# A four-block kernel on one core: the last 107 row transfers of the second expert layer, paced by a pause in place of a count of finished products

## The chip, the cores and the metric

One core of one Trainium2 chip, with its engines TensorE (PE, and PEld for weight loads), VectorE (DVE), ScalarE (ACT), GpSimd (POOL) and the queue engine SyncE (SP). The metric is the device time of one execution in microseconds. All arithmetic is in float32.

## The reference, cut to what matters

An activation x of 32 x 256 tokens with 128 features goes through four residual blocks, each behind a layer norm: a graph layer with gates, an expert layer with one expert of eight per token, a graph layer with two mixings and four small LSTMs of 1 to 4 steps, and an expert layer with two experts of eight per token. The change lies in the last one:

```
logits = flat @ router_w.T
probs = softmax(logits)
topk_probs, topk_idx = top_k(probs, 2)
topk_probs = topk_probs / (sum(topk_probs) + 1e-09)
h1 = einsum('nc,ehc->neh', flat, w1)
h3 = einsum('nc,ehc->neh', flat, w3)
h = silu(h1) * h3
y = einsum('neh,ech->nec', h, w2)
out = einsum('ne,nec->nc', gates, y)
x = x + out
```

Only the two chosen experts of a token are computed by the kernel.

## The kernel before, in words

The 8192 tokens are 64 tiles of 128 and stay in SBUF as `X`. In the second expert layer each token is written twice, once per chosen expert, into the DRAM table `expert_in`, sorted by expert. The table has 136 tiles of 128 rows (`NS` = 136), here called slots, in 17 groups of eight (`ND2` = 17).

The work on slot i:

- SP loads a group of eight slots (L537). TensorE transposes it in two halves (L1434), ACT copies the halves out (L964).
- TensorE makes six products, the two up projections in three parts each (L1444), and signals `d2_h`: one for each slot.
- ACT puts the SiLU on the first projection (L1034) behind a wait on `d2_h`, and copies the weights of a slot four further on (L957). The expert's number is read from a table (L951).
- DVE multiplies with the second projection (L2245) and signals `d2_m`; TensorE's up products of slot i + 2 wait for that (they use the same PSUM banks), and so do the down products of slot i (L1454).
- The result, scaled by the token's gate, is copied out of PSUM by ACT for the first 52 slots (L1000) and by DVE for the others (L2174). Either signals `d2_yo`. It stands in a ring of seven buffers `yd` of eight slots each.
- POOL sends the slot home: an indirect DMA (L712, `rows_home`) scatters its 128 rows of 512 bytes into the DRAM table `expert_out`, each to the place of its token.

At last SP reads that table back in ten blocks (L556), DVE adds the two rows of each token to `X` (L2202), and SP stores the result (L562). The first blocks are read when the groups that can hold their rows are home (`d3_ready`: 11, 13 and 17 groups).

POOL's instructions for this layer are in the order in which they are written. It sends rows 0 to 23 home, writes 32 x 2 half tiles of the second batches of tokens into `expert_in` around rows 24 to 28 (L731, `rows_in(1)` and `rows_in(2)`), and then sends rows 29 to 135 home: the 107 transfers of the change. Two kinds of gates set their times. Each has its own wait, for `d2_yo` to reach i + 1. Beside it the loop holds each one until the layer's progress `d2_h` has reached `min(68 + 5 * (i - 29) // 8, 136)`; 68 is `HOME_REST`. Other loops of indirect transfers have such counts too: L731 in this layer without anything else, the transfers of the first expert layer (L677, L706) and of the LSTM stretch (L687) with a `pause()` between the count and the transfer.

```
def pause():
    step(pool.memset(pause_p[:, :], 0.0))
```

`step` adds a signal to the instruction and lets POOL wait for it. The pause is a memset of one element in each partition (L659).

Of the kernel before, what the change touches and what calls it, by code (L numbers as in the profile page):

```python
# [55 lines left out]
def build(nc, x, adj_t, bias_io, gate_w, gate_b, w1, b1, wg, bg, wd, bd, g0_w, g0_b, g1_w, g1_b, wih_t, whh_t, bih, bhh,  # L56
# [30 lines left out]
    with ExitStack() as ctx:  # L87
# [3 lines left out]
        def sem(name):  # L91
            return ctx.enter_context(nc.semaphore(name))
# [200 lines left out]
        def flat(v):  # L293
# [50 lines left out]
        LG_AT = {i + 1: g for i, g in R_AT.items()}  # L344
        ROUTE_AT = {1: 16, 2: 32}
        RANK_STEP, RANK_COPY_STEP = 4, 5
        HOME_FIRST, LN_AT, IN_AT, HOME_MORE, HOME_REST = 24, (3, 7), (27, 48), 29, 68


        ND2 = NS // 8  # L350
# [4 lines left out]
        d2_tr, d2_xt, d2_h, d2_silu, d2_m, d2_y, d2_yo = (  # L355
            sem("d2_" + n) for n in "tr xt h silu m y yo".split())
# [225 lines left out]
        def _(pool):  # L582
            def step(ins):
                ins.then_inc(pool_step, 1)
                n_pool[0] += 1
                pool.wait_ge(pool_step, n_pool[0])
# [71 lines left out]
            def pause():  # L658
                step(pool.memset(pause_p[:, :], 0.0))  # L659
# [50 lines left out]
            def rows_home(i):  # L710
                pool.wait_ge(d2_yo, i + 1)
                pool.indirect_dma_start(  # L712
                    out=expert_out, out_offset=bass.IndirectOffsetOnAxis(ap=slot_row[:, i:i + 1], axis=0),
                    in_=yd[i // 8 % RING][:, i % 8, :], in_offset=None).then_inc(d2_out[i // 8 % RING], 16)
# [29 lines left out]
                rows_home(i)  # L744
            rows_in(2)
            for i in range(HOME_MORE, 8 * ND2):
                pool.wait_ge(d2_h, min(HOME_REST + 5 * (i - HOME_MORE) // 8, 8 * ND2))
                rows_home(i)


# [1 line left out]
        def _(act):  # L752
# [197 lines left out]
            def load_experts(first):  # L950
                _, r = nc.values_load_multi_w_load_instructions(  # L951
                    tile_e[0:1, bass.ds(first, 1)], engines=[ACT_ENGINE], min_val=0, max_val=E - 1,
                    skip_runtime_bounds_check_because="clamped to the last expert where it is computed")
                return r[0]
# [103 lines left out]
        def _(pe):  # L1058
            def load_experts(first, n):
                _, r = nc.values_load_multi_w_load_instructions(  # L1060
                    tile_e[0:1, bass.ds(first, n)], engines=[PE_ENGINE], min_val=0, max_val=E - 1,
                    skip_runtime_bounds_check_because="clamped to the last expert where it is computed")
                return r
# [447 lines left out]
        def _(dve):  # L1511
# [506 lines left out]
            def b2_dve(g, k, u, first, last):  # L2018
                if isinstance(g, int) and g == NB2 - 1:
                    g_norm(0, 0)  # L2020
                    g_norm(0, 1)
                _, er = nc.values_load_multi_w_load_instructions(
                    tile_e[0:1, bass.ds(4 * g, 4)], engines=[DVE_ENGINE], min_val=0, max_val=E - 1,
                    skip_runtime_bounds_check_because="clamped to the last expert where it is computed")
                dve.wait_ge(b2_y, g + 1)
                if not known_below(g, 2):
                    dve.wait_ge(b2_out[u], 16 * k)
                for j in range(4):
                    ins = dve.tensor_tensor(yb[u][:, j, :], bank[6 + u][:, j * P:(j + 1) * P],
                                            bd_sb[:, bass.ds(er[j] * D, D)], ALU.add)  # L2030
                ins.then_inc(b2_yo, 1)

                ahead_of_end = NB2 - g if isinstance(g, int) else NB2
                if 2 <= ahead_of_end <= 5:
                    for t in range((5 - ahead_of_end) * NH // 4, (6 - ahead_of_end) * NH // 4):
                        b3_tile(t)
                if ahead_of_end == 2:
                    b3_finish(0)
# [275 lines left out]
```

## Time and profile before

| what | us |
|---|---|
| median of three runs | 1142.44 |
| lowest, highest | 1140.64, 1149.63 |
| the profiled execution's own time | 1131.68 |
| its span | 1129.8 |
| TensorE busy in the span | 1019.6 |
| POOL busy in the span | 500.0 |

The profile is of one execution and its times are microseconds from the start of the span. A row of the timeline names start, duration, engine, line of the kernel, operation, what is written and read, the count of merged instructions, and in brackets the idle time of the engine before it with what ended it. "issue" there is time in which the engine waited for nothing that the profile shows, "remote" a releaser that the profile could not name. The ends of matmuls are modelled. A row of the windows names a stretch, its length, the busy time of each engine asked for with the count of its instructions, then TensorE's granted clock as a share of full speed, the share of the DMA engines, and GB/s.

### The profile page before, as it was taken

Reading aid. Unit: us, or ns where it says so; the run is one execution under the profiler, and the core shown is the slowest. Engines: PE = TensorE matmul, PEld = TensorE weight load, DVE = VectorE, ACT = ScalarE, POOL = GpSimd, SP = SyncE. Lnnn points to the kernel's source line nnn. Section 1 sums busy time; section 2 is a strip of 40 time slices with the busy share of each in tenths; the row PEclk is TensorE's granted clock in tenths of the full one; section 3 lists DMA queues with packets and bytes.
Section 4 is the critical chain, followed back from the end, with each engine's and each line's share of the span. In section 5 each row is a group of like instructions: output and inputs, shape, how many; then the busy total and the mean of one; then the engine's idle time right before and its main releaser. Section 6 shows DMA issues by size and latency. Waiting matters only on the chain.

```text
span 1129.8 us, 17682 instructions
## 1 busy us (share of the span) xinstructions
PE 1019.6 (90%) x5432; PEld 714.9 (63%) x5433; DVE 600.5 (53%) x1829; ACT 617.1 (55%) x1158; POOL 500.0 (44%) x831
## 2 busy tenths in 40 slices
PE   5799985999898899999999999999997899989893
PEld 2344432677667544654685456448997798889892
DVE  7977894411165265654765774436474533333365
ACT  4677852544332485664336766656766555454550
POOL 5852275731734420000120058745346666666652
PEclk9899987999998999999999999999998899999997
DMA  9850012332323130000000001131112222222447
GB/s 276 350 221 1 0 45 64 96 105 70 104 68 84 32 119 0 1 1 0 1 1 1 1 31 46 49 86 37 44 46 64 65 83 66 81 63 84 186 159 223
DMA packets 79876, 86.29 MB, mean 76 GB/s; under 512 B 10114, under 2 KB 65970, under 8 KB 79026
## 3 DMA queue, kind: packets, MB, share of 16 engines
q1 hardware_dynamic: 67250, 59.28, 16.6%
q0 software_dynamic: 12544, 25.98, 7.0%
q8 instruction: 44, 0.72, 0.3%
q14 instruction: 38, 0.31, 0.1%
HBM read 40.64 MB, written 44.58 MB: 75 GB/s over the span
## 4 chain that ended last, share of the span: by engine, by line
PE 65%; DVE 13%; ACT 7%; another core or an unknown queue 6%; issue 5%; DMA 2%; POOL 1%; ACTq 1%; DVEq 0%; POOLq 0%; SPq 0%
PE bank L1417 16%; PE bank L1444 14%; PE bank L1424 8%; PE bank L1454 4%; PE bank L1293 3%; PE bank L1181 3%; PE bank L1152 2%; PE bank L1333 2%; PE bank L1361 2%; ACT sb_whh_sb L957 2%; PE bank L1118 1%; PE bank L1322 1%; PE bank L1350 1%; ACTq L951 1%
## 5 line engine op out<-in xcount | busy, mean ns | idle before, releaser
L1417 PE MATMUL bank<-sb_R,sb_wih_sb 128*128 128x512 f32 (+2 forms) x504 | 197.8, 543 | 1.2 <-issue 1.2
L977 ACT ACTIVATE sb_R<-bank,sb_lb_sb 128x512 f32<-128x512 f32 (+2 forms) x252 | 153.4, 634 | 73.7 <-PE bank L1424 61.3
L712 POOL DMA_INDIRECT expert_out<-sb_R,sb_slot_row x136 | 132.5, 974 | 114.6 <-ACT sb_R L1000 45.9
L2245 DVE TENSOR_TENSOR sb_R<-sb_R,bank 114x384 f32<-114x384 f32 x136 | 75.3, 554 | 183.4 <-ACT sb_R L1034 113.0
L1417 PEld LDWEIGHTS bank<-sb_R,sb_wih_sb 128*128 128x128 f32 x504 | 95.3, 190 | 96.4 <-issue 75.7
L1034 ACT ACTIVATE sb_R<-bank 114x384 f32<-114x384 f32 x136 | 66.4, 488 | 148.1 <-PE bank L1444 109.3
L1444 PE MATMUL bank<-sb_xt,sb_wih_sb 128*114 128x128 f32 x792 | 103.4, 282 | 22.4 <-DVE sb_R L2245 9.4
L1454 PE MATMUL bank<-sb_BIG,sb_R 114*128 x816 | 115.5, 278 | 1.3 <-issue 0.8
L1444 PEld LDWEIGHTS bank<-sb_xt,sb_wih_sb 128*114 128x114 f32 x792 | 94.3, 184 | 27.5 <-issue 25.1
L1424 PE MATMUL bank<-sb_R,sb_whh_sb 128*128 128x512 f32 (+2 forms) x288 | 111.1, 529 | 0.0
L1444 PE MATMUL bank<-sb_xt,sb_whh_sb 128*114 128x128 f32 x792 | 99.3, 275 | 5.7 <-ACT sb_wih_sb L957 5.7
L1454 PEld LDWEIGHTS bank<-sb_BIG,sb_R 114*128 114x128 f32 x816 | 103.2, 194 | 1.8 <-issue 1.6
L614 POOL TENSOR_TENSOR sb_ln_p<-sb_ST 128x8 f32<-128x8 f32 (+2 forms) x15 | 3.3, 221 | 221.6 <-DVE sb_ST L1659 162.3
L1444 PEld LDWEIGHTS bank<-sb_xt,sb_whh_sb 128*114 128x114 f32 x792 | 91.8, 179 | 7.9 <-issue 6.9
L659 POOL MEMSET sb_pause_p<- 128x1 f32 x192 | 21.6, 112 | 168.9 <-DVE sb_dest_i L1769 66.4
L901 ACT ACTIVATE sb_R<-bank,sb_b_sb 128x512 f32<-128x512 f32 x72 | 46.3, 688 | 83.3 <-PE bank L1152 75.0
L1424 PEld LDWEIGHTS bank<-sb_R,sb_whh_sb 128*128 128x128 f32 x288 | 54.7, 190 | 50.5 <-issue 35.6
L731 POOL DMA_INDIRECT expert_in<-sb_R,sb_dest_i x64 | 62.1, 970 | 40.4 <-PE bank L1444 17.3
L687 POOL DMA_INDIRECT expert_in<-sb_R,sb_dest_i x64 | 66.5, 1039 | 19.4 <-POOL sb_pause_p L659 11.8
L1293 PE MATMUL bank<-sb_BIG,sb_R 128*128 x576 | 67.8, 276 | 6.4 <-ACT sb_R L901 4.0
L1293 PEld LDWEIGHTS bank<-sb_BIG,sb_R 128*128 128x128 f32 x576 | 65.8, 192 | 8.0 <-issue 7.8
L677 POOL DMA_INDIRECT sorted_in<-sb_R,sb_dest_i x64 | 62.6, 978 | 17.8 <-issue 11.1
(308 smaller groups left out, 1757.6 us busy)
## 6 DMA issues: line engine op xcount, KB each, us to landing
sb_XS<-expert_in SPq DMA_DIRECT2D x17, 528.0 KB
expert_in<-sb_R SPq DMA_DIRECT2D x17, 512.0 KB, 6.3
sb_R<-expert_out SPq DMA_DIRECT2D x6, 1024.0 KB, 6.6
sorted_in<-sb_R SPq DMA_DIRECT2D x9, 512.0 KB, 5.3
sb_XS<-sorted_in SPq DMA_DIRECT2D x18, 256.0 KB
sorted_out<-sb_R SPq DMA_DIRECT2D x18, 256.0 KB
sb_X<-x SPq DMA_DIRECT2D x8, 512.0 KB, 7.5
out<-sb_X SPq DMA_DIRECT2D x6, 512.0 KB
```

Source lines behind the costliest of these rows:

```text
L677: pool.indirect_dma_start(out=sorted_in, out_offset=bass.IndirectOffsetOnAxis(ap=dest_i[:, 0, t:t + 1], axis=0), in_=XN[:, t, :], in_offse ...
L687: pool.indirect_dma_start(out=expert_in, out_offset=bass.IndirectOffsetOnAxis(ap=dest_i[:, k, t:t + 1], axis=0), in_=XR[:, t, :], in_offse ...
L712: pool.indirect_dma_start(out=expert_out, out_offset=bass.IndirectOffsetOnAxis(ap=slot_row[:, i:i + 1], axis=0), in_=yd[i // 8 % RING][:, ...
L731: pool.indirect_dma_start(out=expert_in, out_offset=bass.IndirectOffsetOnAxis(ap=dest_i[:, k, t:t + 1], axis=0), in_=XR[:, t - NH, :], in_ ...
L977: act.activation(gb[s][k][:, 0:c], bank[4 * s + k][:, 0:c], funcs[k], bias=lb_sb[:, (p - 1) * GATES + k:(p - 1) * GATES + k + 1]).then_inc ...
L1034: act.activation(sl[j % 2][0:HC, :], bank[2 + 2 * (j % 2)][0:HC, 0:KU * P], ACT.Silu).then_inc(d2_silu, 1)
L1293: mm = pe.matmul(bank[6 + u][:, j * P:(j + 1) * P], Ht[u][:, c, j * P:(j + 1) * P], wd_sb[:, c, bass.ds(er[j] * D, D)], start=(c == 0 and ...
L1417: mm = pe.matmul(bank[4 * s + k][:, 0:c].rearrange("p (w b) -> p w b", b=GH), wih_sb[:, p - 1, k * P:(k + 1) * P], xin, start=True, stop=( ...
L1424: pe.matmul(bank[4 * s + k][:, 0:c], whh_sb[:, p - 1, k * P:(k + 1) * P], hst[s][:, 0:c], start=False, stop=True).then_inc(l_g, 1)
L1444: mm = pe.matmul(bank[2 + 2 * (j % 2) + part][0:HC, c * P:(c + 1) * P], weights_of(i)[:, part * UP + c * HC:part * UP + (c + 1) * HC], xt[ ...
L1454: mm = pe.matmul(bank[6 + j % 2][:, 0:D], hm[j % 2][0:HC, c * P:(c + 1) * P], down_sb[0:HC, bass.ds(expert * (KU * D) + c * D, D)], start= ...
L2245: dve.tensor_tensor(hm[j % 2][0:HC, :], sl[j % 2][0:HC, :], bank[3 + 2 * (j % 2)][0:HC, 0:KU * P], ALU.mult).then_inc(d2_m, 1)
```

## The change

The wait of each of the last 107 transfers for `d2_h` is taken away, with its constant. In its place stands a `pause()` ahead of the transfers 29 to 119; the last sixteen, 120 to 135 (`8 * (ND2 - 2)` is 120), have none. The wait for the own row, inside `rows_home`, stays.

```diff
--- before.py
+++ after.py
@@ -344,7 +344,7 @@
         LG_AT = {i + 1: g for i, g in R_AT.items()}
         ROUTE_AT = {1: 16, 2: 32}
         RANK_STEP, RANK_COPY_STEP = 4, 5
-        HOME_FIRST, LN_AT, IN_AT, HOME_MORE, HOME_REST = 24, (3, 7), (27, 48), 29, 68
+        HOME_FIRST, LN_AT, IN_AT, HOME_MORE = 24, (3, 7), (27, 48), 29
 
 
         ND2 = NS // 8
@@ -744,7 +744,8 @@
                 rows_home(i)
             rows_in(2)
             for i in range(HOME_MORE, 8 * ND2):
-                pool.wait_ge(d2_h, min(HOME_REST + 5 * (i - HOME_MORE) // 8, 8 * ND2))
+                if i < 8 * (ND2 - 2):
+                    pause()
                 rows_home(i)
```

On POOL's queue the place behind the last of the transfers into `expert_in` (L731) reads as follows. `expert_out` is the table of results, `sb_R` the ring of rows, and the names in brackets are the semaphores waited for; the lines with a minus are the kernel before.

```order
 L731 DMA expert_in<-sb_R,sb_dest_i 17408x132 [waits d2_h,d1_places]
 L731 DMA expert_in<-sb_R,sb_dest_i 17408x132 [waits d2_h] x31
-L712 DMA expert_out<-sb_R,sb_slot_row 33792x128 [waits d2_yo,d2_h] x107
+L659 MEMSET sb_pause_p 128x1
+L712 DMA expert_out<-sb_R,sb_slot_row 33792x128 [waits d2_yo,pool_step]
+L659 MEMSET sb_pause_p 128x1
+L712 DMA expert_out<-sb_R,sb_slot_row 33792x128 [waits d2_yo,pool_step]
```

The 107 transfers that stood as one row with a wait for `d2_h` are now pairs of a memset, which waits for nothing, and a transfer, which waits for the memset and for its own row.

At the end of POOL's queue, the last rows before its final branch are:

```order
+L659 MEMSET sb_pause_p 128x1
+L712 DMA expert_out<-sb_R,sb_slot_row 33792x128 [waits d2_yo,pool_step]
+L659 MEMSET sb_pause_p 128x1
+L712 DMA expert_out<-sb_R,sb_slot_row 33792x128 [waits d2_yo,pool_step]
+L712 DMA expert_out<-sb_R,sb_slot_row 33792x128 [waits d2_yo] x16
 L87 UNCONDITIONAL_BRANCH
```

The sixteen last transfers keep only the wait for their own row. The order of the instructions on the other four engines is as before.

## Rows read from the trace of the kernel before

**Rows 1.** The page: span, busy time by engine, the chain by line

```profile
span 1129.8 us, 17682 instructions
PE 1019.6 (90%) x5432; PEld 714.9 (63%) x5433; DVE 600.5 (53%) x1829; ACT 617.1 (55%) x1158; POOL 500.0 (44%) x831
PE bank L1417 16%; PE bank L1444 14%; PE bank L1424 8%; PE bank L1454 4%; PE bank L1293 3%; PE bank L1181 3%; PE bank L1152 2%; PE bank L1333 2%; PE bank L1361 2%; ACT sb_whh_sb L957 2%; PE bank L1118 1%; PE bank L1322 1%; PE bank L1350 1%;
```

**Rows 2.** Windows, SiLUs of the layer (L1034): us, ACT busy (count), clock, DMA

```profile
946.80:1090.00 143.20, 28.73 (x59) 1.00 0.30 100
```

**Rows 3.** Timeline: first transfer concerned, and SiLUs 67, 126 and 135

```profile
946.80 0.96 POOL L712 DMA_INDIRECT expert_out<-sb_R,sb_slot_row  x1 [1.10 <-PE bank L1444]
946.87 0.49 ACT L1034 ACTIVATE sb_R<-bank 114x384 f32<-114x384 f32 x1 [1.90 <-PE bank L1444]
...
1090.05 0.47 ACT L1034 ACTIVATE sb_R<-bank 114x384 f32<-114x384 f32 x1
...
1108.09 0.49 ACT L1034 ACTIVATE sb_R<-bank 114x384 f32<-114x384 f32 x1 [1.49 <-PE bank L1444]
```

**Rows 4.** Timeline of one burst, 1027 to 1032 us

```profile
1027.83 1.54 PE L1444 MATMUL bank<-sb_xt,sb_wih_sb 128*114 128x128 f32 x12 [1.47 <-ACT sb_whh_sb L957]
1029.04 0.96 POOL L712 DMA_INDIRECT expert_out<-sb_R,sb_slot_row  x1 [0.30 <-issue]
...
1031.10 0.96 POOL L712 DMA_INDIRECT expert_out<-sb_R,sb_slot_row  x1 [1.11 <-PE bank L1444]
1031.18 0.49 ACT L1034 ACTIVATE sb_R<-bank 114x384 f32<-114x384 f32 x1 [2.39 <-PE bank L1444]
```

**Rows 5.** Timeline without bursts, 1092 to 1094 us

```profile
1092.24 1.50 PE L1444 MATMUL bank<-sb_xt,sb_wih_sb 128*114 128x128 f32 x12
...
1094.11 0.49 ACT L1034 ACTIVATE sb_R<-bank 114x384 f32<-114x384 f32 x1 [0.86 <-PE bank L1444]
```

**Rows 6.** 841 to 851 us: windows of transfers (L731), of SiLUs (L1034); timeline

```profile
841.50:851.00 9.50, 7.31 (x8) 0.96 0.15 50
841.50:851.00 9.50, 0.98 (x2) 0.96 0.15 50
...
849.98 0.49 ACT L1034 ACTIVATE sb_R<-bank 114x384 f32<-114x384 f32 x1 [5.61 <-remote]
```

**Rows 7.** Windows to 946.8 us: rows out by ACT (L1000), by DVE (L2174)

```profile
755.00:946.80 191.80, 18.97 (x52) 0.95 0.20 60
755.00:946.80 191.80, 4.47 (x13) 0.95 0.20 60
```

**Rows 8.** Timeline with paused transfers, first expert layer, 172 to 176 us

```profile
172.32 0.11 POOL L659 MEMSET sb_pause_p<- 128x1 f32 x1
172.71 0.96 POOL L677 DMA_INDIRECT sorted_in<-sb_R,sb_dest_i  x1 [0.28 <-issue]
...
174.93 0.60 ACT L836 ACTIVATE sb_R<-bank 128x512 f32<-128x512 f32 x1 [6.45 <-remote]
175.58 0.69 PE L1209 MATMUL bank<-sb_ident,sb_R 128*128 128x128 f32 x2 [6.43 <-issue]
```

**Rows 9.** Timeline of the last transfer, and the chain behind it

```profile
1113.49 0.96 POOL L712 DMA_INDIRECT expert_out<-sb_R,sb_slot_row  x1 [0.30 <-issue]
1113.49 3.65 DMA expert_out<-sb_R,sb_slot_row
...
1117.39 4.25 DMA sb_R<-expert_out
```

**Rows 10.** Windows, a product of the first expert layer (L1181): PE, PEld, clock, DMA

```profile
111.70:152.30 40.60, 23.61 (x48) 7.57 (x46) 1.00 0.04 13
154.20:183.00 28.80, 11.60 (x20) 3.93 (x18) 0.70 0.20 66
```

**Rows 11.** LSTM stretch: windows (PE, PEld, DVE, ACT, POOL); POOL's transfers in lines

```profile
671.00:729.00 58.00, 58.00 (x179) 33.62 (x178) 26.47 (x48) 35.99 (x66) 45.79 (x80) 1.00 0.14 47
L687 POOL DMA_INDIRECT expert_in<-sb_R,sb_dest_i x40 | 41.3, 1032 | 12.0 <-POOL sb_pause_p L659 7.6 <-issue 4.4
```

## The prediction

> **What bounds the kernel now.** Read first the header of the page and the busy time of the last layer's stretches. TensorE is busy 1019.6 of 1129.8 us [rows 1]. The change touches only POOL's last 107 transfers, which run from 946.8 us on, so the question is what sets the pace of the second expert layer from there to the end. The chain of waits over the span puts 14% on L1444, the up product of this layer [rows 1]: TensorE's chain through the slots is what ends last, not POOL.
>
> Then count slots. One slot of 128 rows is one SiLU on ACT at L1034. Between 946.8 and 1090.0 us there are 59 of them [rows 2], and the last ten of the 136 come after. By the starts of slots 67, 126 and 135 (946.87, 1090.05 and 1108.09 us, [rows 3]) 59 steps take 143.2 us, 2.43 us each, and the last nine 18.0 us, 2.00 us each. TensorE's clock is granted in full meanwhile (1.00, its 2.4 GHz level, [rows 2]), so the 0.43 us per slot are waiting: 59 x 0.43 = 25 us.
>
> Where do they go? The timeline of a burst shows it [rows 4]. POOL issues three transfers 1.26 us apart (0.96 for one and 0.30 between), the third at 1029.04. The up product that starts at 1027.83 is over by about 1029.3, yet ACT, idle, starts its SiLU only at 1031.18, after 2.39 us of idleness. POOL, which waits for the same count of finished up products, is let go at 1031.10. So the signal of that product came at about 1031, some 1.7 us late and about 1 us after POOL's third transfer was done (1029.04 + 0.96 = 1030.00). This comes again in each burst. Where POOL sends one or two transfers and then rests, the product at 1092.24 (1.50 us) is answered at 1094.11, 0.4 us after its end [rows 5]. I call it a hold: during transfers in a row TensorE's signals reach nobody, and TensorE, which may be two slots ahead, then stands too. What bounds this stretch is TensorE's chain, and POOL's bursts stretch it. The price of a long burst without pauses is at 841 us: eight transfers in 10 us, beside them two SiLUs, and ACT idle for 5.61 us until 849.98 [rows 6].
>
> **The change, step by step.** *Removed:* POOL's wait for finished up products. At transfer 29 it asks for 68, the next ones for five more in every eight transfers, so bursts of three or four per two slots. At about transfer 125 the rule asks less than the row's own readiness does, and the wait is empty; that is the stretch after 1090. *Kept:* each transfer waits for its own row. Before 946.8 ACT and DVE have put out 52 + 13 = 65 rows [rows 7] and POOL has sent 29 home, so 36 rows are ready: for 36 transfers and more nothing at all stops POOL now.
>
> *Added:* 91 pauses (transfers 29 to 119), a memset of 0.11 us and its own signal. In the paused transfers of the first expert layer the spacing is 1.35 us (0.96 + 0.11 + 0.28, [rows 8]) against 1.26 us without. On POOL that is 91 x 0.09 = 8 us of issue, beside the layer's work as long as POOL is not last. 91 x 1.35 + 16 x 1.26 = 143 us is the least POOL needs; it now takes from 946.80 to 1113.49 + 0.96 = 1114.45, 167.7 us [rows 3, 9].
>
> *Moved:* every one of the transfers 30 to about 124 goes earlier. No other instruction moves on POOL, SP, PE, ACT or DVE. SP's first reads of the rows home wait until transfer 87 has landed, which would be some 946.8 + 59 x 1.35 + 3.65 = 1030 us; they write a region that nobody uses by then, and DVE adds what they bring at fixed slots (the first with 17 slots to go), so I cost their being earlier at nothing. The ring of seven row buffers gets emptier; at a lead of 36 of its 56 rows it was not full before either.
>
> Now the sum. The layer goes through two phases. In phase A POOL runs without stop at 1/1.35 = 0.741 transfers per us and eats its lead of 36 while slots take s us: A = 36 / (0.741 - 1/s). Then it sends one transfer per slot, as after 1090, and slots take 2.00 us. With 68 slots left, the stretch takes T = A + 2.00 x (68 - A/s). Now it takes 143.2 + 18.0 = 161.2 us. So all hangs on s, the slot under transfers with pauses and no stop, which no row shows in this layer. Bounds:
> - s = 2.00, a pause ends every hold: the layer takes 136 us, POOL with 143 us is last, and the end comes 167.7 - 143 = 25 us earlier.
> - s without end, nothing passes before POOL stands: T = 48.6 + 136 = 184.6, 23 us later.
> - s = 2.70 gives 161.2 back: no change.
> Nearest rows. (a) First expert layer, paused transfers in a row from 141 us on: the first product L1181 comes 48 times in 40.6 us before 152.3 us and 20 times in 28.8 us after 154.2 us [rows 10], 0.85 against 1.44 us, a factor 1.7; part of it is a clock of 0.70, itself from TensorE's idling. In it TensorE stands 6.43 us at 175.58 and ACT 6.45 us at 174.93, while POOL's paused transfers run on [rows 8]. 1.7 x 2.00 gives s = 3.4 and T = 169.1. (b) The burst of eight without pauses in this layer gives two SiLUs in 10 us [rows 6], s = 5, T = 175.9. (c) The 40 paused transfers of the LSTM stretch, 671 to 729 us, during which TensorE is busy 58.00 of 58.00 us [rows 11]: no hold at all, s = 2.00. Its products are long and two signals per slot do not hang on each other so tightly.
> I take s = 4, between (a) and (b): pauses were there in (a) and did not help, and this layer's chain leaves TensorE only two slots ahead, so it is nearer to (b) than an estimate by (a) says. A = 36 / 0.491 = 73.3 us, 18.3 slots, T = 73.3 + 99.4 = 172.7, which is 11.5 us more than 161.2. The tail from the last row home (3.65 us to land, 4.25 us to read, adds and stores, [rows 9]) stays. The span goes from 1129.8 to 1141.3 and the profiled execution from 1131.7 to 1143.2 us. That execution lies 10.8 us under the median of the runs, 1142.4; I add the same 11.5 us to the median: 1153.9, put as 1154.
>
> *A rule weighed.* The row shows ACT and TensorE idle beside POOL's transfers and let go when they stop [rows 4]. The Trainium skill, page "SBUF — State Buffer", section "Who interferes with whom", says that DMA never contends with a compute engine and that PE and ACT never wait on anyone. By that rule there is no hold, and the change could only take a wait off POOL, the first rival below. This case's trace disagrees as far as signals go, with 2.39 us of idleness in one burst; it doesn't say that SBUF ports are the cause.
>
> **Rivals.**
> 1. *The pause works* (faster). A memset and a wait on its own signal between two transfers leaves the signals a door, and the hold never forms, as in the LSTM stretch [rows 11]. Against it stand (a) and the 6.4 us [rows 8]. Then s = 2.0 to 2.4: T = 143 to 155, 6 to 25 us less; I price it at 18 less, 1124.
> 2. *Even trade* (no change). Holds form but open by themselves every three or four transfers, s = 2.4 to 2.9: T from 155 to 165, and the 0.43 us saved in phase B pay for phase A. 1142, give or take 6. For it: two slots per burst now already give 2.43.
> 3. *Whole hold* (slower, more). No signal passes until POOL has used up its 36 rows: 48.6 us of standstill at 947 us, then 136 us: 1142 + 23 = 1165. For it: the bursts so far ended only when POOL stopped [rows 4]. Against it: at 849.98 and 174.93 the answer came while transfers ran [rows 6, 8].
> The side changes at s = 2.70.
> 4. That the change does nothing, the own row's wait taking the old wait's place at once, is excluded by the lead of 36 rows [rows 7].
>
> **Chances.** Forecast (s = 3 to 5, 5 to 15 us more): 0.45. Rival 1: 0.27. Rival 2: 0.18. Rival 3: 0.10. One per cent, 11.4 us, is about what a measurement of this kernel can tell from no change. Faster by over 1%: the larger part of rival 1, 0.23. Slower by over 1%: half and more of the forecast and all of rival 3, 0.44. Same: 0.33. The range reaches to 1120 (rival 1 nearly whole) and 1167 (rival 3 with a little over it); the forecast's own is 1147 to 1158.
>
> **What would show it.** Right: SiLUs from 947 us on in pairs with gaps of 5 us and more for some 70 us, some 18 slots in it; POOL's transfers 1.35 us apart with only 0.28 us idle; then slots of 2.00 us with one transfer each; the last SiLU near 1119 us. TensorE's idle time would sit in the first phase, and perhaps its clock falls to the lower level there, which the sum leaves out. Wrong, if slots are at 2.0 to 2.4 us right after 947 us (the pause works), if POOL waits for rows before 1000 us, or if the last transfer is late by itself, with the layer over by 1083 us and POOL still issuing.

## The result, and the profile after

| | kernel before | changed kernel |
|---|---|---|
| median | 1141.54 us | 1168.84 us |
| lowest to highest | 1137.81 to 1149.63 | 1162.08 to 1172.53 |
| ratio, 95% interval | | 1.024 [1.020, 1.028] |
| profiled execution's own time, span | 1131.68, 1129.8 | 1170.66, 1168.4 |

The changed kernel is slower by 2.4%, 27 us. The forecast was 1154, and its range ended at 1167. In the changed kernel the lines of the code stand one higher: L1034 is now L1035, L1444 is L1445, L2245 is L2246. POOL's lines keep their numbers.

The page of the changed kernel, against [rows 1]: span, busy time, the chain by engine, and the SiLUs' group.

```profile
span 1168.4 us, 17757 instructions
PE 1022.7 (88%) x5432; PEld 719.7 (62%) x5433; DVE 601.2 (51%) x1829; ACT 620.8 (53%) x1158; POOL 514.2 (44%) x922
...
PE 58%; DVE 12%; another core or an unknown queue 10%; POOL 7%; issue 6%; ACT 5%; DMA 2%; ACTq 0%; DVEq 0%; SPq 0%; POOLq 0%
...
L1035 ACT ACTIVATE sb_R<-bank 114x384 f32<-114x384 f32 x136 | 66.7, 490 | 174.5 <-PE bank L1445 98.8
```

TensorE does the same work, 1022.7 us against 1019.6, in a span that is 38.6 us longer: the time is waiting. A tenth of the chain (6% before) has no releaser that the profile can name; since the kernel has one core, that is a signal recorded long after the instruction that sent it.

Where it sits, by windows of 20 us of the changed kernel (busy time and count of PE, PEld, DVE, ACT, POOL, then clock, DMA share, GB/s):

```profile
940.00:960.00 20.00, 15.21 (x133) 14.54 (x131) 5.21 (x16) 8.70 (x16) 13.44 (x19) 1.00 0.26 75
960.00:980.00 20.00, 4.34 (x19) 4.11 (x20) 1.70 (x5) 1.16 (x2) 15.83 (x31) 0.59 0.14 47
980.00:1000.00 20.00, 6.00 (x22) 4.70 (x22) 0.01 (x1) 0.00 (x0) 15.45 (x29) 0.59 0.14 49
1000.00:1020.00 20.00, 10.60 (x74) 10.63 (x75) 4.32 (x14) 6.49 (x12) 9.10 (x19) 0.64 0.09 30
1020.00:1040.00 20.00, 20.00 (x184) 20.00 (x183) 8.32 (x25) 12.68 (x23) 10.56 (x20) 1.00 0.30 81
```

From 960 to 1000 us POOL alone works steadily. TensorE is busy 4 and 6 us of 20, and its granted clock is at the lower of its two levels for most of that time (0.59 on average); from 1020 us on it is busy all the time at full clock. The ACT timeline of the same stretch, against [rows 3]:

```profile
957.91 0.49 ACT L1035 ACTIVATE sb_R<-bank 114x384 f32<-114x384 f32 x1 [4.84 <-remote]
...
970.82 0.49 ACT L1035 ACTIVATE sb_R<-bank 114x384 f32<-114x384 f32 x1 [11.77 <-remote]
...
1001.84 0.49 ACT L1035 ACTIVATE sb_R<-bank 114x384 f32<-114x384 f32 x1 [29.86 <-issue]
...
1009.08 0.49 ACT L1035 ACTIVATE sb_R<-bank 114x384 f32<-114x384 f32 x1 [6.09 <-remote]
```

ACT stands idle 4.84, 11.77 and 29.86 us ahead of three SiLUs. Not all of an idle time is a late signal: the up product behind the SiLU at 1001.84 was over only at 982.69, so the SiLU came 19.1 us after it. VectorE waits too. The SiLU at 970.82 is over at 971.31, and its product comes 7.8 us later:

```profile
979.12 0.55 DVE L2246 TENSOR_TENSOR sb_R<-sb_R,bank 114x384 f32<-114x384 f32 x1 [16.36 <-remote]
```

VectorE needs two signals there, ACT's and TensorE's `d2_y` of an earlier down product, and the trace's own record of signals tells them apart. That `d2_y` is recorded at 979.02, 12.2 us after the end of its down product (966.81) and 0.1 us ahead of VectorE's row. Between 940 and 1010 us the trace has 12 signals of ACT and 8 of VectorE (it misses some), and each is recorded 0.01 us after the end of its instruction. Of TensorE's 17, 15 are recorded over 0.5 us late. So it is TensorE's signals that come late, to ACT, to VectorE and, in [rows 4], to POOL.

Nor is it signals alone. The six parts of the down product that comes last before the SiLU at 1001.84 wait for nothing that the profile shows, and yet come one at a time, the starts mostly 0.7, 1.4 or 2.1 us apart. The whole takes 8.1 us, where the six before it, also at the lower clock, took 1.49 us:

```profile
965.32 1.49 PE L1455 MATMUL bank<-sb_BIG,sb_R 114*128 x6
...
987.44 0.37 PE L1455 MATMUL bank<-sb_BIG,sb_R 114*128 x1 [1.84 <-issue]
988.17 0.37 PE L1455 MATMUL bank<-sb_BIG,sb_R 114*128 x1 [0.35 <-issue]
...
990.28 0.37 PE L1455 MATMUL bank<-sb_BIG,sb_R 114*128 x1 [1.74 <-issue]
...
995.20 0.37 PE L1455 MATMUL bank<-sb_BIG,sb_R 114*128 x1 [1.05 <-issue]
```

Meanwhile POOL, in the groups by line between 954 and 1006 us, waits for nothing but its own pauses (count | busy, mean ns | idle before):

```profile
L712 POOL DMA_INDIRECT expert_out<-sb_R,sb_slot_row x38 | 36.4, 957 | 11.5 <-issue 8.7 <-POOL sb_pause_p L659 2.8
L659 POOL MEMSET sb_pause_p<- 128x1 f32 x37 | 4.2, 113 | 0.0
```

At last the SiLUs alone, in the hold and in full flow:

```profile
954.19:1007.20 53.01, 1.47 (x3) 0.62 0.19 59
1017.70:1099.50 81.80, 19.19 (x40) 1.00 0.23 65
```

The sum of the stretch: the first of the 107 transfers goes at 954.19 (before: 946.80, so this execution was 7.4 us later ahead of the change's place), three slots pass until 1007, the fourth SiLU is at 1009.08, and the last one at 1146.86. That is 54.9 + 137.8 = 192.7 us, against 161.3 before: 31.4 us more. The tail behind the last SiLU is 21.5 us against 21.7. So 7.4 + 31.4 - 0.2 = 38.6 us, the difference of the two spans; the medians lie 27.3 us apart.

### The profile page after: what moved, and what is told of

The parts are those of the page before. It is cut to its first block, busy times and chain, and to the rows that moved or that the text cites. A ratio compares the mean times of both kernels' runs of the same rounds, so it can differ in the third digit from the quotient of the medians.

```text
span 1168.4 us, 17757 instructions
## 1 busy us (share of the span) xinstructions
PE 1022.7 (88%) x5432; PEld 719.7 (62%) x5433; DVE 601.2 (51%) x1829; ACT 620.8 (53%) x1158; POOL 514.2 (44%) x922
## 4 chain that ended last, share of the span: by engine, by line
PE 58%; DVE 12%; another core or an unknown queue 10%; POOL 7%; issue 6%; ACT 5%; DMA 2%; ACTq 0%; DVEq 0%; SPq 0%; POOLq 0%
PE bank L1445 14%; PE bank L1418 10%; PE bank L1455 7%; POOL expert_in L687 6%; PE bank L1425 4%; PE bank L1153 4%; PE bank L1294 3%; PE bank L1182 3%; PE bank L1334 2%; PE bank L1362 2%; PE bank L1119 1%; PE bank L1323 1%; PE bank L1351 1%; PE bank L1343 1%
## 5 line engine op out<-in xcount | busy, mean ns | idle before, releaser
L712 POOL DMA_INDIRECT expert_out<-sb_R,sb_slot_row x136 | 136.6, 1004 | 131.5 <-DVE sb_R L2175 56.1
L2246 DVE TENSOR_TENSOR sb_R<-sb_R,bank 114x384 f32<-114x384 f32 x136 | 75.3, 554 | 217.6 <-remote 69.9
L1035 ACT ACTIVATE sb_R<-bank 114x384 f32<-114x384 f32 x136 | 66.7, 490 | 174.5 <-PE bank L1445 98.8
L1455 PE MATMUL bank<-sb_BIG,sb_R 114*128 x816 | 118.7, 281 | 9.2 <-issue 8.7
L1445 PE MATMUL bank<-sb_xt,sb_wih_sb 128*114 128x128 f32 x792 | 105.2, 286 | 23.5 <-DVE sb_R L2246 18.9
L1445 PE MATMUL bank<-sb_xt,sb_whh_sb 128*114 128x128 f32 x792 | 100.4, 277 | 27.4 <-DVE sb_R L2246 13.8
L1445 PEld LDWEIGHTS bank<-sb_xt,sb_wih_sb 128*114 128x114 f32 x792 | 97.9, 189 | 25.3 <-issue 23.3
L1455 PEld LDWEIGHTS bank<-sb_BIG,sb_R 114*128 114x128 f32 x816 | 105.9, 197 | 10.2 <-issue 10.1
L1445 PEld LDWEIGHTS bank<-sb_xt,sb_whh_sb 128*114 128x114 f32 x792 | 93.6, 182 | 29.1 <-issue 29.1
L659 POOL MEMSET sb_pause_p<- 128x1 f32 x283 | 31.8, 112 | 172.7 <-DVE sb_dest_i L1770 72.6
L902 ACT ACTIVATE sb_R<-bank,sb_b_sb 128x512 f32<-128x512 f32 x72 | 46.7, 687 | 82.7 <-PE bank L1153 70.7
L1425 PEld LDWEIGHTS bank<-sb_R,sb_whh_sb 128*128 128x128 f32 x288 | 54.7, 190 | 50.5 <-issue 36.4
L731 POOL DMA_INDIRECT expert_in<-sb_R,sb_dest_i x64 | 62.0, 969 | 43.8 <-PE bank L1445 18.3
L1182 PE MATMUL bank<-sb_xt,sb_w_sb 128*128 128x512 f32 x128 | 69.0, 636 | 4.7 <-ACT sb_R L831 4.4
```

The costliest lines, as they stand in the source:

```text
L712: pool.indirect_dma_start(out=expert_out, out_offset=bass.IndirectOffsetOnAxis(ap=slot_row[:, i:i + 1], axis=0), in_=yd[i // 8 % RING][:, ...
L731: pool.indirect_dma_start(out=expert_in, out_offset=bass.IndirectOffsetOnAxis(ap=dest_i[:, k, t:t + 1], axis=0), in_=XR[:, t - NH, :], in_ ...
L1035: act.activation(sl[j % 2][0:HC, :], bank[2 + 2 * (j % 2)][0:HC, 0:KU * P], ACT.Silu).then_inc(d2_silu, 1)
L1182: pe.matmul(bank[2 + c % 2][:, :], w1_sb[:, c * P:(c + 1) * P], xt[b // 2 % 2][:, b % 2 * BANK:(b % 2 + 1) * BANK], start=True, stop=True) ...
L1425: pe.matmul(bank[4 * s + k][:, 0:c], whh_sb[:, p - 1, k * P:(k + 1) * P], hst[s][:, 0:c], start=False, stop=True).then_inc(l_g, 1)
L1445: mm = pe.matmul(bank[2 + 2 * (j % 2) + part][0:HC, c * P:(c + 1) * P], weights_of(i)[:, part * UP + c * HC:part * UP + (c + 1) * HC], xt[ ...
```

## Experiments

### Two conditions

One fact came with the first comparison and is needed for all that follows. The kernel before takes two times that lie 61 to 77 us apart. Within a comparison it keeps to one of them, with a spread of 2 to 14 us:

| comparison | chip | kernel before, us | kernels |
|---|---|---|---|
| first, with the result | | 1141.54 | changed |
| A | 5 | 1068.29 | bare, both, gap128, two |
| B | 5 | 1068.20 | before_again, after_again |
| C | 5 | 1144.92 | nopause |
| D | 6 | 1129.08 | bare2, gap128b |
| E | 8 | 1138.68 | two2, both2, mem36, dir36 |
| F | 9 | 1139.39 | gap256, sort2, gath2 |
| G | 7 | 1067.83 | sort2b, combo |

I call them the free condition (A, B, G) and the held one. Chip 5 showed both. Every ratio below is to the kernel before in the same comparison.

### Both kernels again

No edit: each kernel as it stood.

> The kernel before, unchanged, for a trace of it where its time is what the last four runs were compared with (1068.3 us, not 1141.5). Theory C (the holding back of signals while GpSimd issues transfers 1.26 to 1.35 us apart belongs to the chip or the session, not to the kernel): no hold in any row of transfers, every slot of the second expert layer 1.98 us with one of 2.42 in four, mean 2.09, and 1068 us. Theory K (it comes and goes from one execution to the next): holds here too, and times that differ by tens of us between runs.

> The changed kernel, unchanged, compared again. Theory C: no hold here, so nothing is lost: GpSimd needs 91 x 1.35 + 16 x 1.26 = 143 us, about what the layer needs (131 us) plus the tail, and the ratio is that of the version with wait and pause, 1.000 to 1.006. Theory K: a hold of some 50 us at the first 36 transfers and a ratio near 1.02 as first measured.

Measured: 1068.19 us, and 1071.17, a ratio of 1.0031 [1.0021, 1.0041]. That is theory C and not K, and by comparison C, on the same chip, it is not the chip. The kernel before, in the free condition: all engines from the first transfer to the last SiLU, then the SiLUs alone, against [rows 2].

```profile
906.70:1044.50 137.80, 137.80 (x1255) 137.80 (x1254) 65.86 (x179) 81.99 (x146) 100.73 (x103) 1.00 0.41 136
```

```profile
906.73:1044.50 137.77, 32.61 (x67) 1.00 0.41 136
```

Rows of POOL and ACT from its timeline:

```profile
930.73 0.96 POOL L712 DMA_INDIRECT expert_out<-sb_R,sb_slot_row  x1 [0.30 <-issue]
...
931.94 0.49 ACT L1034 ACTIVATE sb_R<-bank 114x384 f32<-114x384 f32 x1 [0.80 <-PE bank L1444]
931.99 0.96 POOL L712 DMA_INDIRECT expert_out<-sb_R,sb_slot_row  x1 [0.30 <-issue]
...
933.25 0.96 POOL L712 DMA_INDIRECT expert_out<-sb_R,sb_slot_row  x1 [0.30 <-issue]
...
933.92 0.49 ACT L1034 ACTIVATE sb_R<-bank 114x384 f32<-114x384 f32 x1 [0.83 <-PE bank L1444]
```

Transfers stand 1.26 to 1.29 us apart, 92 in a row, and nothing is held: 67 slots, 2.08 us from one SiLU to the next, with TensorE busy all the time. Between the first transfer and the last SiLU the trace has 148 signals of TensorE, and each is recorded within 0.01 us of its instruction's end; in the held execution, from 946.8 to 1090 us, 76 of 115 are over 0.5 us late. The removed wait stopped none of these 92 transfers; it can have stopped only some of the last fifteen, which go at the pace of the slots. Both executions of the kernel before reach their 166th us within 0.3 us of each other; by the starts of ACT's instructions, each beside its like, the held one falls behind wherever indirect transfers come in rows (the first goes at 142 us): 17.5 us by 380 us, 0.9 us in the LSTM stretch, and the rest in the second expert layer: 63.7 us between the spans of 1129.8 and 1066.1.

In the free condition the change costs what POOL's pauses cost. Its last transfer is at 1055.16 against 1049.87, 5.3 us later, the wait behind it is 1.8 us shorter, and the span 3.5 us longer.

### Without wait and without pause

```diff
-                if i < 8 * (ND2 - 2):
-                    pause()
```

> The changed kernel without its 91 pauses: the last 107 transfers of rows home in the second expert layer have neither the wait nor a pause ahead of them, so GpSimd issues them 1.26 us apart, not 1.35. Theory H (a row of such transfers holds back the signals of the other engines as long as it lasts, pause or no pause): the hold lasts from transfer 29 to about 65, 36 x 1.26 = 45 us instead of the 49 to 52 us of the changed kernel, and the time is 0 to 6 us below the changed kernel's, 1162 to 1169 us. Theory P (the pause instruction itself, a write to SBUF, is what holds): the hold is gone and the time is within 5 us of the kernel before, 1137 to 1147 us.

> The version without wait and without pause again, since the kernel before has shown both of its times (1068 and 1145 us) in comparisons an hour apart. Where before takes about 1068 us again: the same as before, as the first time. Where it takes about 1141 to 1145 us: Theory H (the whole lead of 36 transfers holds the signals, pause or none, and only the end of the row lets them go) gives a hold of 36 x 1.26 = 45 us, a first-transfer-to-last-SiLU stretch of about 45 + 8 (what was in flight) + 65 x 2.12 = 185 us and 1160 to 1170 us, ratio 1.015 to 1.025. Theory P (the pauses made it worse): ratio 1.00 to 1.01.

Measured: free 0.9997 [0.9982, 1.0012]; held 1.0247 [1.0205, 1.0288]. In the held one, SiLUs in the lead (windows) and the one that ends the hold (timeline):

```profile
942.30:989.00 46.70, 0.98 (x2) 0.61 0.20 64
```

```profile
994.38 0.49 ACT L1033 ACTIVATE sb_R<-bank 114x384 f32<-114x384 f32 x1 [37.35 <-remote]
```

Two slots in 46.7 us: as in the changed kernel, over 37 transfers 1.26 us apart. Here too TensorE's signals alone are recorded late (12 of 14 between 935 and 1000 us, none of ACT's 13 or VectorE's 7): the product behind the SiLU at 994.38 ended at 969.00, and its signal is recorded 25.0 us later. The changed kernel's loss is that of the wait removed; the pause of one element neither makes the hold nor breaks it. Theory P falls.

### Wait and pause together

```diff
                 pool.wait_ge(d2_h, min(HOME_REST + 5 * (i - HOME_MORE) // 8, 8 * ND2))
+                if i < 8 * (ND2 - 2):
+                    pause()
                 rows_home(i)
```

> The wait of the kernel before and the pause of the changed one together, ahead of the same transfers. Theory H: with the wait the transfers come in twos and singly, such short rows hold nothing, and a pause inside them adds nothing: within 3 us of the kernel before. Theory P (the pause itself is harmful): 91 pauses in the stretch cost at least 0.1 us each, slower by 9 us or more. If, a third way, the pause does some good once rows are short, the 2.4 us slots of the kernel before shrink towards 2.1 us and it is faster by up to 59 x 0.3 = 18 us.

> The wait of the kernel before and the pause together, again. Where before takes about 1068 us: 1.003 again. Where it takes 1129 to 1145 us: if what holds is the third and fourth transfer of a row, and at 1.35 us a row holds as at 1.26 us, slots stay at 2.43 us and the ratio is 0.998 to 1.004; if 0.09 us more between transfers already eases the hold in short rows, up to 59 slots x 0.3 us less, ratio down to 0.985.

Measured: free 1.0032 [1.0019, 1.0044], held 1.0038 [1.0014, 1.0062]. In the held one 68 slots take 169.7 us against 69 in 161.3 before. With short rows the pause brings nothing and costs 4 to 5 us.

### How far apart

The pause is written over more elements (128 or 256 of each partition), or made twice:

```diff
-                    pause()
+                    long_pause()     # pool.memset(pause_p[:, :], 0.0), pause_p of 128 or of 256 columns
```

> The changed kernel with each of the 91 pauses written over 128 elements of each partition instead of one, so that the transfers should be about 1.45 us apart instead of 1.35. Theory T (there is a spacing from which a row of transfers no longer holds the signals; in the LSTM stretch rows 1.40 to 1.49 us apart held nothing): the hold is gone, the stretch from the first of the transfers to the last SiLU is set by the layer or by GpSimd, 68 x 2.1 = 143 us against 91 x 1.45 + 16 x 1.26 = 152 us, so about 10 us faster than the kernel before. Theory H (any row held close together holds, whatever the small gap): the lead of 36 transfers lasts 36 x 1.45 = 52 us plus what the layer gets done, and the time is that of the changed kernel plus 3 to 6 us.

> The version with transfers 1.46 us apart again. Where before takes about 1068 us: 1.012 again. Where it takes about 1141 to 1145 us: Theory T (from some spacing on a row holds nothing; rows 1.35 to 1.49 us apart held nothing in the LSTM stretch, rows 1.26 us apart did) gives slots of 2.12 us from the first transfer on, GpSimd last at 91 x 1.46 + 16 x 1.26 = 153 us, and 8 to 10 us less than before, ratio 0.99. Theory H: a hold of 36 x 1.46 = 53 us, 1168 to 1176 us, ratio 1.02 to 1.03. In between (s slots per us of hold as I had chosen it for the prediction, s = 4) the ratio is 1.01.

> The changed kernel with a wider pause, two of the short ones in a row ahead of each of the 91 transfers: spacing between 1.45 and 1.75 us. Theory T: no hold; the slots are 2.1 us from the start, the layer ends about 143 us after the first transfer, and GpSimd ends last if the spacing is 1.74 us (91 x 1.74 + 16 x 1.26 = 178 us, 17 us slower than before) or with the layer if it is 1.45 us. Theory H: the hold lasts 36 transfers, 52 to 63 us, and the time is at least that of the changed kernel.

> Transfers 1.84 us apart, again. Where the kernel before takes about 1068 us: ratio 1.045 again. Where it takes 1129 to 1145 us: if the hold gets less with the spacing (1.26 and 1.35 us: no slot gets through; 1.46 us: one in 3.8 us), slots here take 2.1 to 2.4 us from the first transfer on, GpSimd ends last, 192 us from first to last transfer against 167 us before, ratio about 1.02. If spacing does not matter beyond 1.46 us: slots of 3.8 us in the lead, and 1.03 or more.

> The changed kernel with each of the 91 pauses written over 256 elements of each partition: about 1.60 us between transfers. Where the kernel before takes 1129 to 1145 us: if the hold ends below 1.60 us, slots of 2.12 us from the first transfer on, GpSimd last after 91 x 1.60 + 16 x 1.26 + some 4 us for the columns' steps = 170 us against 166.7 us before, ratio 1.000 to 1.003. If it ends between 1.60 and 1.84 us: slots of 2.5 to 3.8 us in the lead, 1.003 to 1.015. Where it takes about 1068 us: GpSimd last, 170 against 143 us, ratio 1.025.

The SiLUs of the layer, windows in the lead, of the versions with 128 columns, with 256, and with two pauses, all held:

```profile
940.30:1024.00 83.70, 10.76 (x22) 0.86 0.21 65
```

```profile
948.29:980.00 31.71, 5.91 (x12) 0.95 0.27 78
948.29:1103.50 155.21, 33.51 (x69) 0.99 0.37 121
```

```profile
950.17:1060.00 109.83, 25.58 (x53) 1.00 0.24 71
```

| spacing, us | kernel | slot in the lead, held | ratio, held | ratio, free |
|---|---|---|---|---|
| 1.26 | bare | 2 in 46.7 us | 1.0247 [1.0205, 1.0288] | 0.9997 [0.9982, 1.0012] |
| 1.35 | changed | 3 in 53.0 us | 1.024 [1.020, 1.028] | 1.0031 [1.0021, 1.0041] |
| 1.46 | gap128 | 3.80 us | 1.0149 [1.0112, 1.0185] | 1.0125 [1.0098, 1.0151] |
| 1.57 | gap256 | 2.64 us | 0.9994 [0.9966, 1.0022] | not tried |
| 1.84 | two | 2.07 us | 1.0180 [1.0132, 1.0227] | 1.0447 [1.0419, 1.0474] |

The hold is a matter of spacing. Below 1.4 us two or three slots get through in some 50 us, at 1.46 a slot takes nearly twice its time, at 1.84 it takes what it takes in the free condition. The other side of it is POOL: at 1.84 us it ends last, at 1144.49 in the held run, 45 us behind the last SiLU, and so at every spacing from 1.35 on in the free condition, where the end comes 14.4 to 14.7 us behind the last transfer. (In both versions with two pauses one slot waits 8 to 14 us: DVE's addition L2204, ahead of the slot's product in its order, waits for rows that POOL sends so late.) Theory H, any close row holds alike, falls. Theory T was right in kind, but not at 1.46, where I had put the end of the hold from the LSTM stretch.

### What in the row holds

The changed kernel with transfers 29 to 64, the lead, replaced. Both leave those rows of the result out; two copies in the LSTM stretch fill them.

```diff
+                if HOME_MORE <= i < HOME_MORE + 36:      # mem36
+                    for k in range(4):
+                        step(pool.memset(pause_p[:, :], 0.0))    # 256 columns
...
+                if HOME_MORE <= i < HOME_MORE + 36:      # dir36
+                    pool.dma_start(out=dump[(i - HOME_MORE) * P:(i - HOME_MORE + 1) * P, :],
+                                   in_=yd[i // 8 % RING][:, i % 8, :]).then_inc(d2_out[i // 8 % RING], 16)
```

> The changed kernel, in which transfers 29 to 64 of the rows home (the 36 of the lead) are left out and four writes of 256 elements of GpSimd's own, each waited for, stand in their place, so that GpSimd stays about as busy but moves nothing; two copies in the LSTM stretch fill the rows that are then not written. Theory D (the transfers hold the signals): no hold in the lead, slots of 2.0 to 2.1 us from the first on also where the kernel before takes 1129 to 1145 us, and 12 to 50 us less than the changed kernel there, ratio to before 0.97 to 0.99. Theory B (GpSimd busy without a stop holds them, whatever it does): the hold of 45 to 52 us remains, ratio about 1.02.

> The changed kernel, in which the same 36 transfers go with the same bytes from the same buffers, on GpSimd's queue, but to rows in order of a buffer of their own instead of the rows that an index names; the same two copies fill the rows not written. If scattering by index is what holds: no hold in the lead, ratio to before 0.97 to 0.99 where before takes 1129 to 1145 us. If any transfer that GpSimd issues holds: as the changed kernel, ratio about 1.02. Where before takes about 1068 us all of this shows nothing and the ratio is 1.00 to 1.01.

Measured, both held: 1.0236 [1.0196, 1.0276] and 1.0063 [1.0025, 1.0100]. By the ratio alone mem36 would be theory B; the windows say otherwise. SiLUs of mem36 beside the memsets and from the first indirect transfer on, then one of its ACT rows there:

```profile
965.00:1023.50 58.50, 13.71 (x28) 1.00 0.16 40
1023.50:1070.00 46.50, 2.45 (x5) 0.65 0.18 58
```

```profile
1061.13 0.49 ACT L1049 ACTIVATE sb_R<-bank 114x384 f32<-114x384 f32 x1 [18.95 <-remote]
```

SiLUs of dir36 beside the direct transfers and after them, and POOL's group of direct transfers:

```profile
964.70:999.60 34.90, 8.33 (x17) 1.00 0.38 117
999.60:1036.00 36.40, 3.43 (x7) 0.72 0.14 45
```

```profile
L715 POOL DMA_DIRECT2D dump<-sb_R x36 | 19.5, 541 | 11.2 <-POOL sb_pause_p L661 11.2
```

Beside POOL's own writes (1.35 us busy of each 1.63) slots take 2.09 us, and beside direct transfers, 36 in 34.9 us with a DMA share of 0.38, 2.05 us. (Windows of this length miss part of a slot; from SiLU to SiLU both are 2.1 us.) As soon as the indirect ones begin, 1.35 us apart, the signals are held: five slots in 46.5 us, seven in 36.4. The hold had only moved: behind the replaced part 34 indirect transfers went without a stop in mem36 and 21 in dir36, against 38 in the changed kernel. That fits the ratios. So what holds, in the held condition, is the row of indirect transfers, not POOL being busy and not DMA traffic. The direct transfers differ from the indirect ones in more than one thing (0.54 us of POOL against 0.96, targets in order), and I did not part these.

### The pauses already there, and rows of the sort

nopause takes the pauses of the kernel before out; sort2 doubles them ahead of the rows that the sort scatters and gathers, gath2 of the gathered ones alone; combo is sort2 and gap256 together.

```diff
             def pause():
-                step(pool.memset(pause_p[:, :], 0.0))
+                pass                                 # nopause
...
                     pause()
+                    pause()                          # sort2: in scatter_b and gather; gath2: in gather
```

> The kernel before without any of its 192 pauses (ahead of the rows scattered in the sort, the rows gathered and the rows scattered in the LSTM stretch); everything else, the wait for the layer's progress too, as before. Theory C (transfers in a row hold nothing where the kernel before takes 1068 us, and something where it takes 1141 us): where before takes 1068 us, the pauses buy nothing, GpSimd is not last in those stages, and the time is within 3 us of before. Where before takes 1141 us, the rows of 1.26 us hold at least as much as those of 1.35 us did (17.4 us lost by the sort's stage), so the same or slower. Theory Q (the pauses already in the kernel are what keeps the signals going where it takes 1068 us): slower than before by 10 us or more, also there.

> The kernel before with two pauses instead of one ahead of each of the 64 rows that the sort scatters and the 64 that it gathers, 1.84 us apart instead of 1.35; the second expert layer as before. Where before takes 1129 to 1145 us: the holds between 150 and 350 us, which cost 17 us, go; against it stands GpSimd's own time, 64 x 0.49 = 31 us more in a stage of 105 us, if the layer has to wait for its rows. Between 17 us less and 14 us more; I take 5 us less, ratio 0.995. Where before takes about 1068 us: 0 to 14 us more.

> The same for the gathered rows alone (64 of them, the first 32 in a row). Where before takes 1129 to 1145 us: the 8 us of hold between 277 and 325 us go and nothing waits for the gathered rows soon after, ratio 0.993; if the gathers are not what held there, 1.000. Where before takes about 1068 us: 1.000.

> The kernel before with two pauses ahead of each scattered and gathered row of the sort, again. Where before takes 1129 to 1145 us: ratio 0.993 as the first time (0.990 to 0.997). Where it takes about 1068 us, where no row holds anything: the rows come 0.16 us later each, 64 x 0.16 = 10 us in a stage that has room for it or not, ratio 1.000 to 1.009.

> Both: two pauses in the sort, and in the second expert layer no wait but a pause of 256 elements (transfers 1.57 us apart). Where before takes 1129 to 1145 us: the sort's gain alone, since GpSimd ends last in the second layer whatever the layer does, 0.9934 x 0.9994 = 0.993; if the two add more than that, because the layer and GpSimd now end close together, 0.985. Where it takes about 1068 us: GpSimd last, 1.025.

nopause, held: 1.0155 [1.0085, 1.0225]. Rows 1.26 us apart now hold in the LSTM stretch too, where rows from 1.35 us on had held nothing [rows 11]: windows of all engines, TensorE 51.78 of 60 us.

```profile
660.00:720.00 60.00, 51.78 (x162) 31.75 (x161) 25.72 (x55) 28.16 (x56) 38.74 (x39) 0.91 0.13 43
```

By the starts of ACT's instructions, each beside the same one of the free execution, this version loses 17.3 us in that stretch and the kernel before 0.9. There 0.09 us of pause are worth some 16 us, while the same pause in the second expert layer is worth nothing. nopause was not tried in the free condition, so theory Q stays untested. sort2 (1.51 us apart): held 0.9934 [0.9897, 0.9971], free 1.0111 [1.0095, 1.0126]. gath2, held: 0.9984 [0.9964, 1.0003], no difference. In the profiled execution of sort2 I don't find the gain at its place, TensorE being busy 200.6 us of 145 to 370 us against 199.6 before, so where its 7 us come from stays open. combo, free: 1.0341 [1.0327, 1.0355]; its layer runs at 2.08 us per slot and POOL ends last at 1088.19, 31.6 us behind the last SiLU. I could not try it held. So one version beats both kernels, by 0.7%, in the held condition alone, and it loses 1.1% in the free one.

## Why the prediction was wrong

*What bounds the kernel: right.* TensorE's chain of slots bounds the stretch, held up by its own signals while POOL's rows go out. The free condition shows the size of it: 2.08 us from SiLU to SiLU, against 2.37 in the held one (68 steps in 161.2 us). The prediction put the waiting at 0.43 us per slot over 59 slots, 25 us; measured against 2.09, the step without holds, it is 0.34 us and 20 us.

*The lead of 36: right.* POOL sent 38 transfers 1.35 us apart without waiting, to 1006 us, and then about one for each slot.

*The moved reads, the tail: right.* They cost nothing, 21.5 against 21.7 us.

*The failed step: "I take s = 4, between (a) and (b)".* It measured 3 slots in 53 us, so s was over 17 and the hold as good as whole. That was rival 3, which had a chance of 0.10. The reasoning failed in two places. (b), two SiLUs beside eight transfers [rows 6], was read as a rate. In bare2 and the changed kernel it is a start: two SiLUs come in the first 14 and 17 us of the row and then none for 38 and 31 us, so dividing a short burst by its slots gives a rate that a long row does not have. And (a), the first expert layer, mixes spacings: [rows 10] covers transfers of which some are 1.5 to 1.9 us apart, and the series above shows that this tenth of a microsecond decides. s = 3.8 is what the layer shows at 1.46 us. I had asked whether the pause opens the door, and not how wide the gap must be. The prediction also took a hold to be late signals alone; the traces show TensorE's own instructions slowed as well, 8.1 us for a down product.

*A mis-sized term: "slots take 2.00 us" in phase B.* Nine slots at the layer's end gave it, [rows 3]. They hold one group of transposes, where full flow has one in each four slots. In full flow of the changed kernel 40 steps from SiLU to SiLU, from 1017.77 to 1101.40 us, take 83.6 us, 2.09 each (the window above, which ends ahead of the last of them, makes it look like 2.05); with the slots right behind the hold 65 took 137.8 us, 2.12 each. Against 2.00 that is 8 us. Rival 3 with it is 184.6 + 8 = 192.6 us, and 192.7 was measured; that it fits so closely is luck, since the hold lasted 54.9 us and not 48.6, and three slots got through in it. Rival 3 had been priced at 1165 us, inside the range; the measured median lies 2 us above the range, less than these 8 us.

*Rival 1, the pause works:* not at 1.35 us. Two pauses in a row do it (2.07 us per slot), and then POOL is last: the 143 us that I had as POOL's least belong to a spacing of 1.35, and at 1.84 it needs 194.

*Rival 2, even trade:* not at 1.35 us either. A trade that comes out even is gap256, 1.57 us apart, 0.9994.

*The rule weighed.* Read as the prediction read it, that nothing is held, the rule doesn't fit the held condition: a SiLU came 19.1 us after its product. The Trainium skill, "SBUF — State Buffer", "Who interferes with whom", speaks of SBUF ports; by that rule POOL's own writes would not disturb TensorE or ACT, and neither would direct DMA, and mem36 and dir36 agree with both (2.1 us per slot). The free condition agrees with it altogether. Had I trusted it, I would have said faster, and in neither condition was the changed kernel faster.

*What stays open.* Why an execution is held or free. The kernel, its work to the 166th us and the number and bytes of its DMA packets are the same, and chip 5 showed both. What the chip's other cores did meanwhile is not on record, and no run here tells whether that, or the recording of the trace, has a part in it. Open too is what part of an indirect transfer slows TensorE, and whether its late signals and its slow instructions have one cause.

## What to carry to other kernels

A count that spaces indirect transfers may look like a needless wait, since all its rows are ready, and in the free condition it was one. In the held condition it broke up a long row. Before such a count is taken away, work out how long the backlog behind it is and how far apart the transfers then come. What a short burst costs per transfer does not price a long row; look for the place in the row from which nothing passes. An engine's idle time tells how long it stood and not whose signal was late; the ends of the instructions that feed it do. And where a comparison of the kernel before gives a second time, take its profile there: here the two profiles side by side showed in which stretches the 63.7 us sit.

## What the runs showed of the hardware that I had not expected

- The same kernel has a free and a held condition, 1068 and 1129 to 1145 us, fixed within a comparison, and not bound to a chip.
- Held, TensorE's signals come late while a row of indirect transfers 1.26 or 1.35 us apart goes out on POOL: a SiLU starts 19.1 us after the end of its product (changed kernel), a signal to ACT is recorded 25.0 us late (bare2), signals to VectorE 12.2 and 14.2 us. ACT's and VectorE's own signals that the trace has come 0.01 us after their instruction in the same stretches.
- In such a row TensorE's instructions that wait for nothing can be slow too: a down product took 8.1 us in place of 1.49, and 13.7 us in bare2.
- Slots in the lead, held: at 1.46 us a slot takes 3.80 us, at 1.57 us 2.64, at 1.84 us 2.07. In the LSTM stretch, with longer products, 1.35 us is enough and 1.26 is not.
- Free, 92 such transfers 1.26 to 1.29 us apart hold nothing.
- 36 direct transfers in 34.9 us on POOL's queue hold nothing in the held condition either.
- A pause of one element adds 0.09 us to the spacing, a second one 0.49 in the second expert layer and 0.16 in the sort.
